# Expert results weighted in the experts and summed by accumulating scatters

## The reference

```
x = layernorm(x + attention(x))           # 16 heads of 16, causal, ALiBi, LoRA on q, k, v
probs = softmax(x @ Wg)                    # 8 experts
topv, topi = top_k(probs, 2)
gates = topv / sum(topv)
pos  = running number of the entry within its expert;  keep = pos < cap   (cap = 1076)
slots[e, pos] = x[token]                   # each token goes to two experts
y[e] = gelu(slots[e] @ W1[e] + b1[e]) @ W2[e] + b2[e]      # 256 -> 1024 -> 256
out  = gates[0]*keep[0]*y[first] + gates[1]*keep[1]*y[second]
x = layernorm(x + out)
```

## Time and profile before

| what | value |
|---|---|
| median of 3 runs (lowest, highest) | 1393.92 us (1392.9, 1398.17) |
| the profiled execution: its time, its span | 1393.77 us, 1392.0 us |
| busy share of the span: TensorE, VectorE, ScalarE, GpSimd | 87%, 41%, 67%, 25% |
| bytes moved | 112.11 MB, mean 81 GB/s |
| attention | to about 876 us |
| last block's routing | about 878 to 928 us |
| experts | about 928 to 1327 us |
| combine | about 1331 to 1392 us |

### The profile page before, as it was taken

One profiled execution on the slowest core, in us unless ns is written; L12 is line 12 of the kernel. 1 busy time (PEld: TensorE's weight loads), 2 busy tenths in 40 slices (PEclk: granted clock), 3 DMA queues, 4 the chain that ended last, 5 costly groups with the idle time before them and its releaser, 6 DMA issues. The chain is left out here.

```text
span 1392.0 us, 23705 instructions
## 1 busy us (share of the span) xinstructions
PE 1204.1 (87%) x8566; PEld 499.5 (36%) x8566; DVE 571.9 (41%) x1528; ACT 933.3 (67%) x1227; POOL 350.1 (25%) x424
## 2 busy tenths in 40 slices
PE   7799999999998999989989989329999999999900
PEld 3222212222222212222222211117778778777800
DVE  4232221212023245545444500536545654655457
ACT  2578879888986998989879989125444543543234
POOL 2321211101100132342322220142333243333242
PEclk9899999999998999999999999659999999999955
DMA  6942333232023112411230000523331331200054
GB/s 145 174 105 75 76 94 85 65 78 75 10 78 89 42 56 79 118 62 59 92 101 20 15 17 7 191 79 105 101 107 43 110 105 38 90 25 29 20 201 161
DMA packets 78972, 112.11 MB, mean 81 GB/s; under 512 B 11349, under 2 KB 58245, under 8 KB 78864
## 3 DMA queue, kind: packets, MB, share of 16 engines
q1 hardware_dynamic: 65872, 77.16, 20.2%
q0 software_dynamic: 11616, 32.35, 6.6%
q10 hardware_dynamic: 1376, 1.18, 0.5%
HBM read 60.88 MB, written 52.33 MB: 81 GB/s over the span
## 5 line engine op out<-in xcount | busy, mean ns | idle before, releaser
L1096 ACT ACTIVATE prob<-ps_s 128x1024 f32<-128x1024 f32 (+3 forms) x859 | 721.1, 986 | 116.3 <-PE ps_s L1025 107.7
L1041 PE MATMUL ps_o<-prob,v_aug 128*17 128x512 f32 (+3 forms) x3294 | 441.5, 572 | 17.6 <-DVE acc L1153 5.8
L1025 PE MATMUL ps_s<-qop,kop 51*128 51x512 f16 (+3 forms) x1647 | 279.7, 372 | 34.0 <-ACT prob L1096 9.8
L1025 PEld LDWEIGHTS ps_s<-qop,kop 51*128 51x128 f16 x1647 | 67.5, 93 | 405.4 <-ACT prob L1096 332.3
L1776 PE MATMUL ps_y<-w2s,hs 128*128 128x256 bf16 (+1 forms) x1728 | 199.5, 273 | 0.0
L1760 PE MATMUL ps_h<-xs,w1s 128*128 128x384 bf16 (+1 forms) x1152 | 181.5, 317 | 5.0 <-ACT hid L1823 4.3
L1823 ACT ACTIVATE hid<-ps_h,b 128x384 f32<-128x384 f32 (+1 forms) x192 | 105.1, 560 | 118.9 <-PE ps_h L1760 95.8
L1119 POOL TENSOR_SCALAR_AFFINE_SELECT prob<-prob 128x256 f32<-128x256 f32 (+1 forms) x172 | 68.1, 405 | 440.8 <-ACT prob L1096 438.9
L1776 PEld LDWEIGHTS ps_y<-w2s,hs 128*128 128x128 bf16 (+1 forms) x1728 | 167.4, 99 | 17.5 <-issue 0.2
L1153 DVE COPY acc<-ps_o 64x512 f32<-64x512 f32 x64 | 44.1, 689 | 234.7 <-PE ps_o L1041 227.0
L1760 PEld LDWEIGHTS ps_h<-xs,w1s 128*128 128x128 bf16 x1152 | 111.7, 98 | 69.5 <-ACT hid L1823 7.0
(11 more groups left out here) (149 smaller groups left out, 693.8 us busy)
## 6 DMA issues: line engine op xcount, KB each, us to landing
w<-in_W SPq DMA_DIRECT2D x16, 1024.0 KB, 7.5
ye<-entries_y SPq DMA_DIRECT2D x8, 1024.0 KB, 7.5
slots_x<-empty POOLq DMA_DIRECT2D x12, 516.0 KB, 4.4
entries_y<-empty POOLq DMA_DIRECT2D x12, 512.0 KB
qop<-fparts_q SPq DMA_DIRECT2D x42, 128.0 KB, 4.3
xe<-slots_x SPq DMA_DIRECT2D x8, 645.0 KB
x_all<-in_xT SPq DMA_DIRECT2D x8, 512.0 KB, 5.2
fparts_k<-x_all SPq DMA_DIRECT2D x16, 256.0 KB, 2.2
```

Source lines behind the costliest of these rows:

```text
L1025: mm = pe.matmul(ps_s[:, u.p % SLOTS_S, e, u.q0:], o.key(e, u.i, u.kt), o.query(e, u.i, u.b, u.q0), start=True, stop=True)
L1041: mm = pe.matmul(ps_o[c:c + VW, u.q0:], o.v[:, u.kt, 2 * u.i + e], prob[:, t % RING, n, e, u.q0:], start=u.first, stop=end)
L1096: act.activation(prob[:, t % RING, n, u.heads[0]:2, u.q0:], ps_s[:, u.p % SLOTS_S, u.heads[0]:2, u.q0:], ACT.Exp, scale=1.0 / (SCALE * SCA ...
```

## The change

The router's row grows by two words, the two gates. A block's gates are computed with its routing (`act_gate` on ScalarE at the turns of `GATE_AT`, `weigh` on VectorE at the end of `places`). SP stores each block of `x1_all` to a new array `result` in memory (`store_base`, at `BASE_AT`; the last block in `route_last`). `entries_y`, its clearing, `weight_all` and the combine's sums are gone. In the experts VectorE picks the slot's gate (`entries`), adds the bias into `yb` (which now signals `y_sum`, for which TensorE waits), and multiplies it by the gate into `y`. The scatter adds to the token's row of `result` by the DMA's own add; an expert's first scatter waits for all scatters of the expert before. The end (`Combine`) is in the same block: SP waits for the scatters, loads `result` (512 KB a block), VectorE takes statistics and roots in five groups of blocks (0-1, 2-3, 4-5, 6, 7), with the next group's statistics laid between the steps of the root, and applies half of the last block's rows itself.

```diff
-ROW = D + 2
+
+ROW = D + 4
...
+    BASE_AT[_t + 8] = _n
+    GATE_AT[_t + 8] = _n
...
+                    if t in BASE_AT:
+                        r.store_base(sp, BASE_AT[t])
...
+                    if t in GATE_AT:
+                        r.act_gate(act, GATE_AT[t])
...
-                    if t in CLEAR_Y_AT:
-                        k, a, z = CLEAR_Y_AT[t]
-                        pool.dma_start(entries[k, :, a:z], empty[:, 0:D].unsqueeze(1).broadcast_to([P, z - a, D])).then_inc(y_cleared, 16)
...
+        dve.tensor_tensor(r.gap[:, n % 2], r.top[:, :, 1], r.top[:, :, 0], ALU.subtract).then_inc(r.gap_done, 1)
...
+        r.weigh(dve, n)
+
+    def weigh(r, dve, n):
+
+        dve.wait_ge(r.gexp_done, n + 1)
+        dve.tensor_scalar(r.gsum[:], r.gexp[:, n % 2], 1.0, None, ALU.add).then_inc(r.gsum_done, 1)
+        dve.wait_ge(r.gsum_done, n + 1)
+        first, second = (r.xsplit[:, :, k].rearrange("p (s o) -> p s o", o=1) for k in (D + 2, D + 3))
+        dve.reciprocal(first, r.gsum[:].unsqueeze(2)).then_inc(r.gates, 1)
+        dve.wait_ge(r.gates, 2 * n + 1)
+        dve.tensor_tensor(second, r.gexp[:, n % 2].unsqueeze(2), first, ALU.mult).then_inc(r.gates, 1)
...
+            pool.wait_ge(r.gates, 2 * n + 2)
...
-    def act_gates(r, act):
-        act.wait_ge(r.step, NB * r.STEPS)
-        act.activation(r.gexp[:], r.gap_all[:], ACT.Exp).then_inc(r.gexp_done, 1)
-
-    def dve_gates(r, dve):
-
-        c = Chain(dve, r.g_step, 0, 3)
-        dve.wait_ge(r.gexp_done, 1)
-        c.did(dve.tensor_scalar(r.gsum[:], r.gexp[:], 1.0, None, ALU.add))
-        c.wait()
-        c.did(dve.reciprocal(r.gate[:, :, :, 0], r.gsum[:]))
-        c.wait()
-        c.did(dve.tensor_tensor(r.gate[:, :, :, 1], r.gexp[:], r.gate[:, :, :, 0], ALU.mult))
-        c.wait()
-        c.end()
-        dve.tensor_tensor(r.weight_all[:], r.gate[:].rearrange("p n s k -> p n (s k)"), r.keep_all[:],
-                          ALU.mult).then_inc(r.weights, 1)
+    def act_gate(r, act, n):
+        act.wait_ge(r.gap_done, n + 1)
+        act.activation(r.gexp[:, n % 2], r.gap[:, n % 2], ACT.Exp).then_inc(r.gexp_done, 1)
+
+    def store_base(r, sp, n):
+
+        sp.wait_ge(r.x1_done, (n + 1) * KT)
+        sp.dma_start(r.result.rearrange("(n s p) d -> n p s d", s=KT, p=P)[n], r.x1[:, n]).then_inc(r.base_stored, 16)
...
-                        sp.wait_ge(entry_done, e * 2 + 2)
+                        sp.wait_ge(entry_done, e * 4 + 4)
                         X.load_weights(sp, io, u, e + 2)
                         load(u, e + 2)
+                for k in range(3):
+                    sp.wait_ge(y_stored[k], 16 * (E * ST // 3))
+                z.sync(sp)
...
-                    pool.wait_ge(y_out, e * ST + (k + 1 + 2))
+                    pool.wait_ge(y_out, e * ST + (k + 1))
                     if k == 0:
-                        pool.wait_ge(entry_done, e * 2 + 2)
+                        pool.wait_ge(entry_done, e * 4 + 4)
+                        if not (isinstance(e, int) and e == 0):
+
+                            for v in range(3):
+                                pool.wait_ge(y_stored[v], e * (16 * ST // 3))
                     alone(pool)
                     pool.indirect_dma_start(
-                        out=entries_y, out_offset=bass.IndirectOffsetOnAxis(ap=entry[0:n, u, k:k + 1], axis=0),
-                        in_=y[0:n, k % 3], in_offset=None, bounds_check=2 * T - 1,
-                        oob_is_err=False).then_inc(y_stored[k % 3], 16)
+                        out=result, out_offset=bass.IndirectOffsetOnAxis(ap=entry[0:n, u, k:k + 1], axis=0),
+                        in_=y[0:n, k % 3], in_offset=None, bounds_check=T - 1,
+                        oob_is_err=False, compute_op=ALU.add).then_inc(y_stored[k % 3], 16)
...
+                pool.wait_ge(r.base_stored, 16 * NB)
...
-                        pe.wait_ge(y_out, e * ST + (k + 1))
+                        pe.wait_ge(y_sum, e * ST + (k + 1))
...
+                    bias = b2[0:n, bass.ds(e, 1)].rearrange("p o d -> p (o d)")
+                    dve.tensor_tensor(yb[0:n, k % 2], ps_y[0:n, (ST * u + k) % 2, 0:D], bias, ALU.add).then_inc(y_sum, 1)
                     if not (isinstance(e, int) and e == 0 and k < 3):
 
                         dve.wait_ge(y_stored[k % 3], e * (16 * ST // 3) + (k // 3) * 16)
-                    bias = b2[0:n, bass.ds(e, 1)].rearrange("p o d -> p (o d)")
-                    dve.tensor_tensor(y[0:n, k % 3], ps_y[0:n, (ST * u + k) % 2, 0:D], bias, ALU.add).then_inc(y_out, 1)
+                    dve.wait_ge(y_sum, e * ST + (k + 1 + 2))
+                    dve.tensor_scalar(y[0:n, k % 3], yb[0:n, k % 2], weight[0:n, u, k:k + 1], None, ALU.mult).then_inc(y_out, 1)
...
+                    for n, ks in parts:
+                        mine = X.expert[0:n, bass.ds(e, 1), ks].rearrange("p o k -> p (o k)")
+                        dve.tensor_tensor(same[0:n, ks], xe[0:n, u, ks, D + 1], mine, ALU.is_equal).then_inc(picked, 1)
+                        dve.tensor_scalar(entry[0:n, u, ks], xe[0:n, u, ks, D], 0.5, None, ALU.mult).then_inc(entry_done, 1)
                     for q, (n, ks) in enumerate(parts):
-                        mine = X.expert[0:n, bass.ds(e, 1), ks].rearrange("p o k -> p (o k)")
-                        dve.tensor_tensor(other[0:n, ks], xe[0:n, u, ks, D + 1], mine, ALU.not_equal).then_inc(tag_read, 1)
+                        dve.wait_ge(picked, e * 4 + (q + 1))
+                        dve.scalar_tensor_tensor(out=pick[0:n, ks], in0=same[0:n, ks], scalar=2.0, in1=xe[0:n, u, ks, D + 3],
+                                                 op0=ALU.mult, op1=ALU.add).then_inc(picked, 1)
                     for q, (n, ks) in enumerate(parts):
-                        dve.wait_ge(tag_read, e * 2 + q + 1)
-                        dve.tensor_tensor(entry[0:n, u, ks], xe[0:n, u, ks, D], other[0:n, ks], ALU.add).then_inc(entry_done, 1)
+                        dve.wait_ge(picked, e * 4 + (q + 3))
+                        dve.tensor_tensor(weight[0:n, u, ks], pick[0:n, ks], xe[0:n, u, ks, D + 2], ALU.min).then_inc(entry_done, 1)
...
+class Combine:
+
+
+    GROUPS = [(0, 1), (2, 3), (4, 5), (6,), (7,)]
+    WIDEST = 2
...
+    def sync(z, sp):
+        for n in range(NB):
+            sp.dma_start(z.z[:, n], z.src[n]).then_inc(z.loaded[n], 16)
+        for n in range(NB):
+            sp.wait_ge(z.applied[n], KT)
+            sp.dma_start(z.dst[n], z.z[:, n]).then_inc(z.stored, 16)
+        sp.wait_ge(z.stored, 16 * NB)
+
+    def scalar(z, act):
+        for g, blocks in enumerate(z.GROUPS):
+            act.wait_ge(z.scales, g + 1)
+            for n in blocks:
+                for s in range(KT if g < len(z.GROUPS) - 1 else KT // 2):
+                    act.activation(z.z[:, n, s], z.z[:, n, s], ACT.Identity, scale=z.rstd[:, n, s:s + 1],
+                                   bias=z.nmr[:, n, s:s + 1]).then_inc(z.applied[n], 1)
+
+    def vector(z, dve):
+
+        c = Chain(dve, z.step, 0, RSQRT_STEPS * len(z.GROUPS))
+        d = Chain(dve, z.spread_step, 0, 2 * KT * NB)
+        for s in z.spread(d, 0):
+            pass
+        for g, blocks in enumerate(z.GROUPS):
+            later = z.spread(d, g + 1) if g + 1 < len(z.GROUPS) else iter(())
+            n0, w = blocks[0], len(blocks)
+            mean, var = z.mv[:, n0:n0 + w, :, 0], z.mv[:, n0:n0 + w, :, 1]
+            rstd = z.rstd[:, n0:n0 + w]
+            tmp = [z.tmp[:, k, 0:w] for k in range(5)]
+            d.wait()
+            for k, _ in enumerate(rsqrt_pieces(c, var, tmp, rstd)):
+                if k >= 3:
+                    next(later, None)
+            c.wait()
+            dve.scalar_tensor_tensor(out=z.nmr[:, n0:n0 + w], in0=mean, scalar=-1.0, in1=rstd, op0=ALU.mult,
+                                     op1=ALU.mult).then_inc(z.scales, 1)
+            if g == len(z.GROUPS) - 1:
+                n = blocks[0]
+                for s in range(KT // 2, KT):
+                    dve.tensor_scalar(z.z[:, n, s], z.z[:, n, s], z.mv[:, n, s, 0:1], z.rstd[:, n, s:s + 1],
+                                      ALU.subtract, ALU.mult).then_inc(z.applied[n], 1)
+            for _ in later:
+                pass
+        c.end()
+        d.end()
+
+    def spread(z, d, g):
+
+        dve = d.eng
+        for v, n in enumerate(z.GROUPS[g]):
+            dve.wait_ge(z.loaded[n], 16)
+            for s in range(KT):
+                d.did(dve.bn_stats(z.stats[:, g % 2, v, s], z.z[:, n, s]))
+                yield
+        d.wait()
+        for v, n in enumerate(z.GROUPS[g]):
+            for s in range(KT):
+                d.did(dve.bn_aggr(z.mv[:, n, s], z.stats[:, g % 2, v, s]))
+                yield
...
```

More of the change, by code:

```diff
@@ L258, in build @@
                 route_last(nc, io, psum, r, x)
-                experts(nc, io, psum, slots_x, entries_y, x)
-        combine(nc, io, sb, psum, sem, x1_all, entries_y, weight_all)
```

(52 more changed lines are left out.)

169 lines of the change are left out of this document (41 added, 128 removed).

## The result

The changed kernel takes 1361.55 us (median of 4 runs, 1359.46 to 1366.05) against 1393.41 us (median of 4): ratio 0.9776, 95% interval 0.976 to 0.9793. The forecast was 1366. Timed again on another chip, five runs gave 1354.47 against 1384.22, ratio 0.9777 (0.9764 to 0.9791).

What follows compares the result with a forecast made beforehand. TensorE was taken to bound attention and experts, VectorE's chain the last 67 us. The new end at 1361.0, plus 1.0, 0.6 and 1.5, gave a 1364.1 us span; +1.8 made 1366 us, range 1359 to 1376.

Steps and rivals of the forecast that it cites:

- Attention: Attention stage: seven added Exps of 0.23 us at most, without waits, plus stores, less clearing DMAs; +1.0 us, bounds -1 and +2.5.
- Routing: Last routing before the experts: gates stand ahead of the eight scatters, delaying the first; +0.6 us, bounds 0 and 1.5.
- Experts: Expert stage: added VectorE work mostly covered by idle time, 0.2 us at each of seven boundaries; +1.5 us, bounds 0 and 9.
- my rivals: Alternatives: seam's excess returns 0.12, expert boundaries delay TensorE 0.09, landing doubles 0.12, scatter slow 0.10, everything covered 0.11.
- The scatter: Accumulating scatter: lands 5.0 us from its start, bounds 3.5 and 12.5; costs 0 in the experts, +1.5 at the end.
- the slow scatter: Rival, experts and end: slow landing delays multiplies at seven boundaries; gain gone at 10.8 us, 1410 at 12.5; chance 0.10.
- the doubled landing: Rival, scatter: destination rows fetched like source rows, landing in 7.0 us, 2.0 later at the end, 1368; chance 0.12.
- The ring of three: Experts' three scatter buffers: a landing of up to about 7.5 us makes nothing late.
- the sign that I had named for a wrong forecast: Experts: multiplies standing behind stores would show the forecast wrong.
- The seam: Between experts and end: most of the 8.4 us from last scatter to first load goes, leaving 5.2.
- The end: Final stage: first landing 4.1 us after load, VectorE's chain 23.6, ScalarE's applies fit inside; span ends at 1361.0 before other terms.
- the reading that it is the slowed steps, the 32 adds and the seam that go, and not the bytes: End: halved load bytes give nothing themselves; 32 adds of 0.38 to 0.53 us, slowed small steps and most seam go.

Runs made afterwards that it cites:

- d_unroll: Changed kernel with VectorE's loop over the six middle experts' passes written out, so no jump back there; ratio 0.9765 to the kernel before.
- n_pad: Kernel before with 60 semaphore increments nobody waits for ahead of each expert's pass on VectorE; profile only, pass at the jump 54.87 us.
- h_act: Changed kernel with the multiply by the gate moved from VectorE to ScalarE; ratio 0.9788 to the kernel before.
- b_plain: Changed kernel with the scatter in the experts lacking the DMA's add, so rows overwrite and no sum is formed; ratio 0.9771 to the kernel before.
- c_seam: Changed kernel with its end put into a block of its own behind the experts' block; ratio 0.9805 to the kernel before.
- s_wait: Kernel before with SP instead of GpSimd waiting for the last scatters; profile only, last scatter's start to first load 7.11 us instead of 8.42.
- g_nosum: Kernel before, its combine without GpSimd's add of the token's own row; profile only, first load to end 50.2 us instead of 60.4.
- f_apart: Changed kernel with the next group's statistics behind the root's twelve steps instead of between them; ratio 0.9834 to the kernel before.

## Why the prediction was right

*Attention:* +1.1 in the pair of profiles, +1.0 said. The Exp had no wait ahead, as forecast, but took 0.40 us in attention (median of eight) and not 0.23. With a spread of 13 us in this mark the agreement proves nothing; stores, Exp and missing clears were not separated. They can't be worth much: with the marks behind attention taken off, the medians leave it within a few us of nothing.

*Routing:* +0.9 where +0.6 was said. The gates stand ahead of the scatters:

```profile
916.76 1.00 POOL L1522 DMA_INDIRECT slots_x<-xsplit,dest_all  x1 [4.36 <-DVE xsplit L1500]
...
929.65 0.37 SPq L1702 DMA_DIRECT2D xe<-slots_x  x1
```

The destinations are done at 915.27 and the first scatter starts 1.5 us behind; it was 0.9 at the scatter of 914.76. So the 0.6 is shown; the other 0.3 is within what this stretch varies by.

*Experts:* the step that failed. I took 0.2 us for each of seven boundaries; six cost nothing (the passes are those of before to 0.01 us), since the small instructions and the multiply fit VectorE's idle time. The 5.1 us are one jump (3.15, shown by d_unroll and n_pad), one held multiply (0.7; with the second expert's held too, 1.5; h_act has none), and 1.1 of TensorE's clock, which varies with and without the change. So the change itself cost the experts about 4 us, where 1.5 was said. The jump was in none of my rivals: I costed instructions by their busy time and idle cover, and not by the length of the loop that holds them.

*The scatter:* the landing was mis-sized. 5.0 us from the start was the tile of 128 rows plus a guess for the add; with the add such a tile lands in 3.7 to 4.0 in six of the seven places where a multiply waits for it, as here (start 1126.41, multiply 1130.25), and in 5.2 in the second expert:

```profile
1126.41 1.56 POOL L1733 DMA_INDIRECT result<-y,entry  x1 [0.17 <-issue]
...
1130.25 0.35 DVE L1874 TENSOR_SCALAR y<-yb,weight 128x256 f32<-128x256 f32 x1 [0.94 <-DMA result<-y,entry]
```

The 3.5 worked out for the plain one was too long: one lands in at most 2.9 (b_plain, first expert). So for 128 rows the add costs 1 us or more, 0.57 of it in the issue. And the last tile has only 52 rows, and has landed 1.2 us behind its issue. So neither the slow scatter nor the doubled landing (7.0) happened. The ring of three bore it: multiplies waited 8.4 us in seven places for stores (the sign that I had named for a wrong forecast), and TensorE never for that. The cost that I did not name is GpSimd's issue, 1.56 instead of 0.98 us: it ends the w2 subtraction later, and with it the held multiply, and is nearly all of its 0.7 us (0.14 in b_plain).

*The seam:* it went nearly whole, as the forecast had it: 3.1 of the 5.8 is the boundary (c_seam), 1.3 GpSimd's late wake (s_wait), the rest probably the old start. It gained 2.6 more than said because the last scatter was reckoned at 5.0 us and SP's load starts 2.65 behind its start.

*The end:* 30.3 us where 32.3 were summed up. First landing in 3.5 instead of 4.1, VectorE's chain 22.1 instead of 23.6: a statistic and a small step take 0.41 together, as summed up, but the first aggregate of a group lies free between two steps, and the next root starts 0.03 us behind the last aggregate and not 0.2, about 0.3 a group. That ScalarE's applies fit inside was only just so: from 1349.36 on it has no gap. Of the reading that it is the slowed steps, the 32 adds and the seam that go, and not the bytes, GpSimd's share (10.2, g_nosum) and the seam are shown, and 3.9 are the statistics laid between the steps (f_apart). VectorE's 32 adds (17.3 us busy before) were not taken out alone. The bytes did give something: the first landing comes 3.53 us behind its issue and not 5.48.

## What to carry to other kernels

Before adding instructions to a loop over a register, look at how long the loop becomes on that engine, not only at how much idle time covers them: in the longer loops here the jump back cost 3 us each time. Writing the passes out on that engine alone took it away; moving the work to another engine moved part of it there. When a stage's idle engine is given work, look for the instruction of the other engine that can hold it, and move the shorter one to an engine that isn't held. Split a gain or loss by marks before naming its cause: here the clock's rise stood in the same pass as the held multiply and was the larger of the two. And compare variants by marks within the trace when the stage ahead of the change spreads by more than the change is worth.

## What the hardware showed that was not expected

An accumulating indirect DMA of 128 rows of 1 KB costs GpSimd 1.56 us instead of 0.98 and lands 3.7 to 4.0 us behind its start (once 5.2), the plain one at most 2.9 (b_plain, first expert). 60 semaphore increments on VectorE's queue hold it for 5.5 to 6.0 us, about 0.1 us each (n_pad). VectorE's jump back costs 3.1 to 3.3 us in seven profiles, the longer loop of before among them. A block boundary whose engines are otherwise ready costs 3.1 us (c_seam). In six profiles the fourth multiply was held for 5.5 us thirteen times, starting 0.67 to 0.76 us ahead of GpSimd's subtraction, and went free 29 times, starting 0.75 to 0.89 us ahead, so the same kernel has it in one expert or in two. TensorE's granted clock rises 6.2 to 9.0 us behind its first instruction of the experts, differently in each run.
